# An eight-core block of convolution, attention and a product layer: work moved between the engines, and layer-norm sums made inside the tile loops

## The chip, the cores and the metric

The kernel runs on the 8 NeuronCores of one Trainium2 chip, each with its own part of the tokens and no traffic between cores. The metric is the device time of the slowest core, in microseconds (us). A core has TensorE (PE; its weight loads are PEld), VectorE (DVE), ScalarE (ACT), GpSimd (POOL) and SyncE (SP), each with its own queue that runs in program order; they wait for one another by semaphores only.

## What is computed

x has 4 x 2048 tokens of 4096 values. The reference, cut to what matters (all biases kept, names shortened):

```python
def attn(x):
    y = conv1d(x, conv_w, width=3, 'SAME') + conv_b        # 4096 -> 3*1024
    q, k, v = split(y, 3)                                  # in blocks of 128 tokens
    qh, kh, vh = q @ wq + bq, k @ wk + bk, v @ wv + bv     # 16 heads of 64
    p = softmax(where(causal, (qh/8) @ kh.T, -1e9))        # within a block
    return ((p @ vh) @ wo + bo) @ proj_w + proj_b          # -> 4096
def ffn(x):
    return x @ W.T + b + sum_e probs[e] * (x @ A[e].T) @ B[e].T   # 16 x rank 16
x = layernorm(x + attn(x))
x = layernorm(x + ffn(x))
```

## The kernel before

Each core takes 1024 tokens (T), held transposed: the 4096 channels are 32 chunks (DC) of 128 partitions, the tokens run along the free dimension in two halves of 512 (TH). All products are bf16, 128x128 weights against 128x512 data into one PSUM bank of eight; `tile_i % 8` picks the bank. Nothing orders the work but the program: `Sched.op` (line 65) appends an instruction to an engine's list with its semaphore waits, so the order in which the Python loops emit is the order of every queue. A DVE or ACT instruction also waits for its predecessor on its own engine. DMAs are issued from POOL (they cast float32 to bf16 on the way) or from SP.

The stages, in order:

- **Convolution** (lines 290 to 337), q/k/v products (349 to 416) and a pre-pass for the softmax maxima (427 to 472). The change leaves these alone.
- **Attention** (474 to 547), eight blocks of 128 tokens, PSUM halves psA and psB in turn. `attn_smm(b)` makes the scores. `attn_chain(b)`: ACT exp (497), DVE mask multiply (501), PE sums by a matmul with ones (507), DVE reciprocal over 128x2048 (513), PE p times v (521), and 16 small DVE multiplies that scale by the reciprocal and write otb (539). Emission is smm(0), smm(1), chain(0), smm(2), chain(1) and so on; smm(b+2) waits for the last otb write of block b, and lies ahead of the ones matmul of block b+1 in PE's queue.
- **P4**, `emit_p4(half)` (560 to 687): 8 tiles of otb times wo (592), then 32 tiles of a1b times proj_w (665), 8 matmuls each. Weights come tile by tile into two buffers, wsA and wsB, by POOL DMA (627); the load of tile n+2 waits for the matmuls of tile n. x comes as float32 into xjit0/1 by SP DMA (643). DVE adds bias and x while it reads PSUM and writes res1 in bf16 (676).
- **LN1**: `emit_ln1_stats` (689): 32 ACT squares (703), and two matmuls with ones for each chunk, the sum (709) and the sum of squares (716). `emit_ln_chain` (726): three ACT instructions, a DVE subtract and a reciprocal, an ACT square root. `emit_ln1_apply` (751): for each chunk a DVE add and a DVE multiply, 64 in all, with float32 negmean and rstd.
- **ht**, `emit_ht(half)` (762): 64 matmuls with A (772), and two DVE evacuations to hb (782).
- Emission around LN1 is p4(0), stats(0), apply(0), the POOL loads of A and B (806, 810), p4(1), ht(0), stats(1), apply(1), ht(1).
- **FFN** (867 to 906): 64 tiles of 34 matmuls (878, 887); DVE adds bias and x1 from PSUM (896); weights by POOL DMA (859).
- **LN2** (919 to 979), for each half in turn: squares (935), ones matmuls (941, 950), the chain, then 32 times a DVE add (967), a DVE multiply (970) and an SP DMA to the output (974), through four ob buffers.

In P4 the order within a tile is:

```python
        for dmc in range(DC):
            ...                       # waits: pw_ld[dmc], a1_done, bank_free[bank]
            for wc in range(WC): ...  # pmm, 8 matmuls on PE
            stream_free[par] = ("tC", S.n("tC"))
            ...
            S.op("vector", pevac, wait=ww)   # ww: the matmuls and xj_ld[dmc]
            if dmc + 2 < DC:
                emit_pw_load(dmc + 2)
                emit_xj_load(dmc + 2)
```

Of the kernel before, what the change touches and what calls it, by code (L numbers as in the profile page):

```python
# [14 lines left out]
D = 4096  # L15
# [35 lines left out]
OFF_SPARE = 206656  # L51


class Sched:
# [41 lines left out]
def build_nc(taps=(), stop_after='full'):  # L96
# [25 lines left out]
    idf_d = dt("idf", (128, 128), F32)  # L122

# [8 lines left out]
    def sb(name, off, shape, dtype):  # L132
# [25 lines left out]
    rstd = sb("rstd", OFF_STATS + 6144, (128, TH), F32)  # L158
    hb = sb("hb", OFF_HBOX, (128, 2048), BF16)
# [29 lines left out]
    xjit0 = sb("xjit0", REG2 + 40960, (128, TH), F32)  # L189
    xjit1 = sb("xjit1", REG2 + 43008, (128, TH), F32)  # L190
# [14 lines left out]
    SEMS = ("xS", "c0", "c1", "w2", "s0", "s1", "sD",  # L205
# [30 lines left out]
    v_prep = S.n("vC")  # L236

# [254 lines left out]
    def attn_chain(b):  # L492
# [8 lines left out]
        S.op("vector", lambda e, pb=pb: e.tensor_mul(  # L501
            pb[:, :], pb[:, :], maskt[:, :]),
            wait=[("cC", st["exp"])])
        st["mask"] = S.n("vC")
        for j in range(4):
            def lmm(e, j=j, ps=ps, pb=pb):
                return e.matmul(ps[:, j * 512:(j + 1) * 512], ones128[:, :],  # L507
                                pb[:, j * 512:(j + 1) * 512],
                                start=True, stop=True)
            S.op("tensor", lmm, wait=[("vC", st["mask"])],  # L510
                 inc="tC" if j == 3 else None)
# [3 lines left out]
        st["recip"] = S.n("vC")  # L515
        for h in range(H):
# [9 lines left out]
            S.op("tensor", omm, wait=[("vC", st["recip"])],  # L526
                 inc="tC" if h == H - 1 else None)
        st["omm"] = S.n("tC")
        for h in range(H):
            def oev(e, b=b, h=h, ps=ps, lv=lv):  # L530
                src = ps[(h % 2) * 64:(h % 2) * 64 + 64,
                         (h // 8) * 512 + ((h // 2) % 4) * 128:
                         (h // 8) * 512 + ((h // 2) % 4) * 128 + 128]
                dst = otb[(h % 2) * 64:(h % 2) * 64 + 64,
                          (h // 2) * 1024 + b * 128:
                          (h // 2) * 1024 + b * 128 + 128]
                lvs = lv[(h % 2) * 64:(h % 2) * 64 + 64,
                         scol(h):scol(h) + 128]
                return e.tensor_mul(dst, src, lvs)  # L539
            S.op("vector", oev, wait=[("tC", st["omm"])])  # L540
        blk_oevac[b] = [("vC", S.n("vC"))]
# [7 lines left out]
    p3_done = [("cC", S.n("cC")), ("vC", S.n("vC")), ("tC", p3_t_done)]  # L549
# [9 lines left out]

    def emit_p4(half):  # L560
        nonlocal tile_i
        hofs = half * TH
        wo_ld = {}
        def emit_wo_load(wc):
# [3 lines left out]
            waits = [("tC", p3_t_done)]  # L568
# [13 lines left out]
        for wc in range(WC):  # L582
            par = wc % 2
            buf = wsA if par == 0 else wsB
            bank = tile_i % 8
# [28 lines left out]
        xj_free = {0: None, 1: None}  # L614

# [15 lines left out]
        def emit_xj_load(dmc):  # L631
# [14 lines left out]
            S.op("sync", xdma, wait=xw, inc=sem, k=16)  # L646
# [6 lines left out]
        res1_writes = []  # L653
        for dmc in range(DC):
# [3 lines left out]
            bank = tile_i % 8  # L658
# [3 lines left out]
            for wc in range(WC):  # L662
                def pmm(e, dmc=dmc, wc=wc, bank=bank, buf=buf,
                        first=(wc == 0), last=(wc == WC - 1)):
# [3 lines left out]
                        start=first, stop=last)  # L668
                S.op("tensor", pmm, wait=waits,
                     inc="tC" if wc == WC - 1 else None)  # L670
                waits = []
            stream_free[par] = ("tC", S.n("tC"))
            t_grp = S.n("tC")
            ww = [("tC", t_grp), xj_ld[dmc]]
            def pevac(e, dmc=dmc, bank=bank, xbuf=xbuf):
                return e.scalar_tensor_tensor(
                    res1_ap(dmc), pbank(bank), projb[:, dmc:dmc + 1],
                    xbuf[:, :], ALU.add, ALU.add)
            S.op("vector", pevac, wait=ww)
            bank_free[bank] = ("vC", S.n("vC"))  # L680
            xj_free[par] = ("vC", S.n("vC"))
            res1_writes.append(S.n("vC"))
# [4 lines left out]
        ln_state[half] = dict(res1=res1_writes)  # L687

    def emit_ln1_stats(half):
        nonlocal tile_i  # L690
        st = ln_state[half]
        b1 = tile_i % 8
        b2 = (tile_i + 1) % 8
        tile_i += 2
        w1 = [bank_free[b1]] if b1 in bank_free else []
        w2w = [bank_free[b2]] if b2 in bank_free else []
        mm2_done = []
        for dc in range(DC):
            sqw = [("vC", st["res1"][dc])]
            if dc >= 2:  # L700
                sqw.append(("tC", mm2_done[dc - 2]))
            def sq(e, dc=dc):
                return e.activation(  # L703
                    sqtmp[:, (dc % 2) * 512:(dc % 2) * 512 + 512],
                    res1_ap(dc), AF.Square)
            S.op("scalar", sq, wait=sqw)
            c_sq = S.n("cC")
            def mm1(e, dc=dc, b1=b1):
                return e.matmul(pbank(b1), ones128[:, :], res1_ap(dc),
                                start=(dc == 0), stop=(dc == DC - 1),  # L710
                                skip_group_check=True)
# [12 lines left out]
        st["b1"], st["b2"], st["t_stats"] = b1, b2, t_stats

    def emit_ln_chain(st):
# [4 lines left out]
        S.op("scalar", lambda e: e.activation(  # L731
            negmean[:, :], pbank(b1), AF.Copy, bias=0.0, scale=-1.0 / D),
# [13 lines left out]
        S.op("scalar", lambda e: e.activation(rstd[:, :], tmp1[:, :],  # L746
                                              AF.Sqrt),
             wait=[("vC", v_r)])
        return S.n("cC")

    def emit_ln1_apply(half):
        st = ln_state[half]
        c_rstd = emit_ln_chain(st)
        for dc in range(DC):
            S.op("vector", lambda e, dc=dc: e.tensor_add(
                res1_ap(dc), res1_ap(dc), negmean[:, :]),
                wait=[("cC", c_rstd)])
            S.op("vector", lambda e, dc=dc, half=half: e.tensor_mul(  # L758
                x1b_ap(half, dc), res1_ap(dc), rstd[:, :]))
        st["applied"] = ("vC", S.n("vC"))  # L760

    def emit_ht(half):
        nonlocal tile_i
        for erc in range(ERC):
            bank = tile_i % 8
            waits = [g_at, ln_state[half]["applied"]]
# [292 lines left out]
```

How the kernel before makes its waits and increments, by code:

```python
        def run(e, sems, fn=fn, waits=waits, inc=inc, k=k):  # L85
            for s, v in waits:
                e.wait_ge(sems[s], v)
            inst = fn(e)
            if inc is not None:
                inst.then_inc(sems[inc], k)
```

## Time and profile before

| | us |
|---|---|
| runs of the kernel before, median of 3 | 2531.28 (2527.34 to 2542.32) |
| the profiled execution, whole | 2560.23 |
| its span on the slowest core (core 7) | 2558.7 |
| spans of the other cores | 2512.8 to 2541.9 |

| stage on core 7 | from, to (us) | length |
|---|---|---|
| convolution, q/k/v, pre-pass | 0 to 1247.5 | 1247.5 |
| attention | 1247.5 to 1443.7 | 196.2 |
| P4 of half 0 (wo; proj_w) | 1443.7 to 1619.8 | 30.9; 145.2 |
| statistics of half 0, wait for weights | 1619.8 to 1648.0 | 28.2 |
| P4 of half 1 (wo; proj_w) | 1648.0 to 1831.0 | 31.0; 152.0 |
| ht(0), LN1 of half 1, ht(1) | 1831.0 to 1945.0 | 114.0 |
| FFN | 1945.0 to 2415.7 | 470.7 |
| LN2 | 2415.7 to 2558.7 | 143.0 |

The page gives PE 76% of the span busy, DVE 19%, ACT 6%, POOL 13%. A row of the timeline is a start, a length, the engine, the line of the kernel, the operation with the names and shapes that it writes and reads, and how many instructions are merged; the bracket tells how long the engine had stood idle and what released it. A matmul's length includes its way through the array, so back-to-back matmuls overlap: 32 of them that last 0.38 us each take 6.9 us. The clock column is the granted TensorE clock as a share of full speed: 1.00 is 2.4 GHz, 0.50 is 1.2 GHz, a value between is a mixture over the stretch.

### The profile page before, as it was taken

To read this page: it belongs to the slowest core of one execution; us is meant where nothing else is said; L and a number is where in the kernel's file an instruction comes from. 1 tells how busy PE (TensorE), PEld (TensorE's weight loads), DVE (VectorE), ACT (ScalarE), POOL (GpSimd) and SP (SyncE) were. 2 spreads that over 40 slices of the span, in tenths; PEclk is the share of its full clock that TensorE was granted. 3 is DMA by queue.
4 is the path that set the end of the run, shared out by engine and by line. 5 is a ranking of instruction groups with operands and counts; after the bars stand their busy time and mean duration, and the time that the engine had idled before them with its cause. 6 is when DMAs were issued, how large, how long until landed. Compare 5 with 4: busy or idle time off the path is not lost.

```text
span 2558.7 us, 20840 instructions; the slowest of 8 cores (2512.8 to 2558.7 us)
## 1 busy us (share of the span) xinstructions
PE 1951.9 (76%) x8634; PEld 831.3 (32%) x8634; DVE 485.8 (19%) x586; ACT 163.6 (6%) x234; POOL 324.1 (13%) x316
## 2 busy tenths in 40 slices
PE   0499999999999999999311355665618999999940
PEld 0244444444444444444200111121203444444300
DVE  0000000000000000001687411261161011011077
ACT  0000000000000000012000000300120000000140
POOL 1112112121121212100000111111100111111000
PEclk9988899999999999999655678877868999999975
DMA  9956888898979797910000378978702878778433
GB/s 144 97 54 57 76 82 78 83 84 77 90 75 96 66 89 66 83 33 1 1 0 0 41 107 115 118 96 121 93 0 24 75 66 74 74 67 76 40 119 144
DMA packets 544385, 184.51 MB, mean 72 GB/s; under 512 B 516131, under 2 KB 520355, under 8 KB 544036
## 3 DMA queue, kind: packets, MB, share of 16 engines
q0 software_dynamic: 524416, 148.93, 60.9%
q1 hardware_dynamic: 19876, 34.25, 4.4%
q8 instruction: 69, 1.13, 0.2%
q14 instruction: 24, 0.20, 0.0%
HBM read 315.29 MB, written 16.78 MB: 130 GB/s over the span
## 4 chain that ended last, share of the span: by engine, by line
PE 71%; DVE 13%; DMA 10%; issue 5%; ACT 1%; POOL 0%; DVEq 0%; POOLq 0%; ACTq 0%
PE psA L304 20%; PE psB L304 20%; PE psA L878 9%; PE psB L878 9%; DVE linv L513 4%; DMA wsB<-projw 3%; DMA wsA<-projw 3%; DMA wsA<-wo 2%; PE psB L665 2%; PE psA L665 2%; DVE ob L967 2%; DVE ob L970 2%; DVE otb L539 1%; PE psA L361 1%; PE psB L361 1%
## 5 line engine op out<-in xcount | busy, mean ns | idle before, releaser
L304 PE MATMUL psA<-xb,cwb 128*128 128x512 bf16 x2304 | 521.8, 391 | 96.3 <-DMA cwb<-cw 96.3
L304 PE MATMUL psB<-xb,cwb 128*128 128x512 bf16 x2304 | 517.0, 388 | 0.0
L304 PEld LDWEIGHTS psA<-xb,cwb 128*128 128x128 bf16 x2304 | 228.7, 99 | 388.0 <-issue 168.5
L304 PEld LDWEIGHTS psB<-xb,cwb 128*128 128x128 bf16 x2304 | 227.6, 99 | 288.4 <-issue 59.2
L267 POOL DMA_DIRECT2D cwb<-cw x144 | 164.8, 1175 | 879.1 <-PE psA L304 436.1
L326 DVE TENSOR_SCALAR qkvb<-psA,convb_s 128x512 bf16<-128x512 f32 x8 | 6.0, 750 | 588.0 <-PE psA L304 588.0
L326 DVE TENSOR_SCALAR qkvb<-psB,convb_s 128x512 bf16<-128x512 f32 x8 | 6.0, 751 | 505.5 <-PE psB L304 505.5
L859 POOL DMA_DIRECT2D wsA<-Wt x32 | 36.5, 1146 | 304.8 <-PE psA L887 213.2
L665 PE MATMUL psB<-a1b,wsA 128*128 128x512 bf16 x128 | 45.3, 518 | 36.8 <-DMA wsA<-projw 35.2
L665 PE MATMUL psA<-a1b,wsB 128*128 128x512 bf16 x128 | 46.1, 525 | 30.3 <-DMA wsB<-projw 30.3
L665 PE MATMUL psA<-a1b,wsA 128*128 128x512 bf16 x128 | 41.1, 479 | 34.8 <-DMA wsA<-projw 33.4
L665 PE MATMUL psB<-a1b,wsB 128*128 128x512 bf16 x128 | 38.8, 457 | 28.8 <-DMA wsB<-projw 28.7
L703 ACT ACTIVATE sqtmp<-res 128x512 bf16<-128x512 bf16 x64 | 40.3, 629 | 317.9 <-PE psA L716 138.5
L859 POOL DMA_DIRECT2D wsB<-Wt x32 | 36.5, 1144 | 190.2 <-PE psA L887 100.7
L878 PE MATMUL psA<-x1bA,wsB 128*128 128x512 bf16 x256 | 56.6, 379 | 1.1 <-DVE res_lo L896 1.1
L878 PE MATMUL psA<-x1bA,wsA 128*128 128x512 bf16 x256 | 56.6, 379 | 1.1 <-DVE hb L782 1.1
L878 PE MATMUL psB<-x1bA,wsB 128*128 128x512 bf16 x256 | 56.6, 379 | 0.0
L878 PE MATMUL psB<-x1bA,wsA 128*128 128x512 bf16 x256 | 56.6, 379 | 0.0
L935 ACT ACTIVATE sqtmp<-res_lo 128x512 bf16<-128x512 bf16 x32 | 20.1, 629 | 543.0 <-PE psA L950 449.1
L772 PE MATMUL psB<-x1bB_lo,atb 128*128 128x512 bf16 x32 | 9.5, 461 | 58.7 <-DVE x1bB_hi L758 58.7
L513 DVE RECIPROCAL linv<-psA 128x2048 f32<-128x2048 f32 x4 | 51.8, 12957 | 8.7 <-PE psA L507 8.7
L513 DVE RECIPROCAL linv<-psB 128x2048 f32<-128x2048 f32 x4 | 51.8, 12957 | 8.7 <-PE psB L507 8.7
(169 smaller groups left out, 1505.8 us busy)
## 6 DMA issues: line engine op xcount, KB each, us to landing
cwb<-cw POOLq DMA_DIRECT2D x144, 512.0 KB, 21.6
xjit<-xT SPq DMA_DIRECT2D x64, 256.0 KB, 3.9
wsA<-Wt POOLq DMA_DIRECT2D x32, 512.0 KB, 10.4
wsB<-Wt POOLq DMA_DIRECT2D x32, 512.0 KB, 10.4
outT<-ob SPq DMA_DIRECT2D x64, 256.0 KB, 2.0
xb<-xT POOLq DMA_DIRECT2D x4, 2052.0 KB, 46.3
wsA<-projw POOLq DMA_DIRECT2D x32, 256.0 KB, 5.7
wsB<-projw POOLq DMA_DIRECT2D x32, 256.0 KB, 5.7
```

The lines of the kernel that those rows point to most:

```text
L267: return e.dma_start(out=dst, in_=src)
L304: return e.matmul(pbank(bank), buf[:, (w * 32 + dc) * 128:(w * 32 + dc + 1) * 128], xb[:, dc * (T + 2) + tokc * 512 + w: dc * (T + 2) + to ...
L361: return e.matmul(pbank(bank), wcs[dc][:, hc * 128:hc * 128 + 128], qkvb[:, (qoff + dc) * 1024 + tokc * 512: (qoff + dc) * 1024 + tokc * 5 ...
L513: S.op("vector", lambda e, ps=ps, lv=lv: e.reciprocal(lv[:, :], ps[:, :]), wait=[("tC", st["lmm"])])
L539: return e.tensor_mul(dst, src, lvs)
L665: return e.matmul(pbank(bank), buf[:, wc * 128:wc * 128 + 128], a1b[:, wc * TH:(wc + 1) * TH], start=first, stop=last)
L703: return e.activation(sqtmp[:, (dc % 2) * 512:(dc % 2) * 512 + 512], res1_ap(dc), AF.Square)
L859: return e.dma_start(out=dst, in_=src)
L878: return e.matmul(pbank(bank), buf[:, dc * 128:dc * 128 + 128], x1b_ap(half, dc), start=first, stop=False)
L935: return e.activation(sqtmp[:, (dc % 2) * 512:(dc % 2) * 512 + 512], res2_ap(dc)[:, hofs:hofs + TH], AF.Square)
L967: S.op("vector", lambda e, dc=dc, slot=slot, hofs=hofs: e.tensor_add(ob[slot][:, :], res2_ap(dc)[:, hofs:hofs + TH], negmean[:, :]), wait=ww)
L970: S.op("vector", lambda e, slot=slot: e.tensor_mul(ob[slot][:, :], ob[slot][:, :], rstd[:, :]))
```

## The change

- Attention: the mask multiply goes from DVE to POOL. After the reciprocal a new POOL multiply scales the 128x2048 probabilities, and p times v waits for it; the 16 DVE writes of otb become 4 ACT copies of 64x512 each.
- P4: x is loaded as bf16 by POOL DMA and added by a ninth matmul with an identity (idb, a new constant). ACT instead of DVE evacuates PSUM. The square and the two ones matmuls of a chunk are emitted right behind its evacuation, so in PE's queue they stand ahead of the next tile's matmuls. `emit_ln1_stats` is gone. Tiles rotate over banks 0 to 3; banks 4 and 5 hold the sums. The first weight and x loads wait for earlier blocks of the attention than before.
- LN1 apply: negmean and rstd are cast to bf16, and 16 DVE instructions on 128x2048 (the row repeated 4 times by `bc3`) take the place of 64 on 128x512.
- FFN: an identity matmul adds x1; ACT evacuates and squares; both ones matmuls stand in PE's queue behind each tile (banks 4 to 7). The first two weight loads are emitted ahead of ht(1).
- LN2: both chains first; then chunk by chunk half 0 on DVE and half 1 on POOL, two ob buffers each; the output DMAs stand in SP's queue in turn.
- POOL instructions wait for their predecessor by a semaphore of their own (gC). The `stop_after` exits are removed.

```diff
+def bc3(ap2d, reps):
+    return dataclasses.replace(ap2d, ap=[ap2d.ap[0], [0, reps], ap2d.ap[1]])
@@ attn_chain
-        S.op("vector", lambda e, pb=pb: e.tensor_mul(
+        S.op("gpsimd", lambda e, pb=pb: e.tensor_mul(
             pb[:, :], pb[:, :], maskt[:, :]),
+            wait=[("cC", st["exp"])], inc="gC")
@@ after the reciprocal
+        S.op("gpsimd", lambda e, pb=pb, lv=lv: e.tensor_mul(
+            pb[:, :], pb[:, :], lv[:, :]),
+            wait=[("vC", st["recip"])], inc="gC")
+        st["pnorm"] = ("gC", S.n("gC"))
-            S.op("tensor", omm, wait=[("vC", st["recip"])],
+            S.op("tensor", omm, wait=[st["pnorm"]],
-        for h in range(H):
-            def oev(...): ... return e.tensor_mul(dst, src, lvs)
-            S.op("vector", oev, wait=[("tC", st["omm"])])
-        blk_oevac[b] = [("vC", S.n("vC"))]
+        for g in range(2):
+            for bot in range(2):
+                def oev(...): ... return e.activation(dst, src, AF.Copy)
+                S.op("scalar", oev, wait=[("tC", st["omm"])])
+        blk_oevac[b] = [("cC", S.n("cC")), ("vC", st["recip"])]
@@ emit_p4
-            S.op("sync", xdma, wait=xw, inc=sem, k=16)
+            S.op("gpsimd", xdma, wait=xw, inc=sem, k=16)
+            def pxadd(e, dmc=dmc, bank=bank, xbuf=xbuf):
+                return e.matmul(pbank(bank), idb[:, :], xbuf[:, :],
+                                start=False, stop=True)
+            S.op("tensor", pxadd, wait=[xj_ld[dmc], sd_idb], inc="tC")
             stream_free[par] = ("tC", S.n("tC"))
-            S.op("vector", pevac, wait=ww)
+            S.op("scalar", pevac, wait=pw_)
             if dmc + 2 < DC:
                 emit_pw_load(dmc + 2)
                 emit_xj_load(dmc + 2)
+            S.op("scalar", sq, wait=sqw)
+            S.op("tensor", mm1, wait=stat_w1 + [("cC", c_evac)], ...)
+            S.op("tensor", mm2, wait=stat_w2 + [("cC", c_sq)], inc="tC")
@@ emit_ln1_apply
-        for dc in range(DC):
-            S.op("vector", ... tensor_add(res1_ap(dc), res1_ap(dc), negmean))
-            S.op("vector", ... tensor_mul(x1b_ap(half, dc), res1_ap(dc), rstd))
+        gate = emit_ln_chain(st, negmean, rstd, make_bf=True)
+        for g in range(8):
+            S.op("vector", lambda e, r=r: e.tensor_add(
+                r, r, bc3(nmb[:, :], 4)), wait=[gate])
+            S.op("vector", lambda e, r=r, xo=xo: e.tensor_mul(
+                xo, r, bc3(rstdb[:, :], 4)))
@@ FFN tile
+            S.op("tensor", fxadd, wait=[sd_idb], inc="tC")
-            S.op("vector", fevac, wait=[("tC", t_grp)])
+            S.op("scalar", fevac, wait=[("tC", t_grp)])
+            S.op("scalar", sq2, wait=sqw)
+            S.op("tensor", mm1, wait=hs["w"][hs["b1"]] + [("cC", c_evac)], ...)
+            S.op("tensor", mm2, wait=hs["w"][hs["b2"]] + [("cC", c_sq)],
+                 inc="tC")
@@ LN2
+    for half in range(2):
+        gate = emit_ln_chain(st, nm_t, rs_t, make_bf=False)
+        apply_specs.append((half, nm_t, rs_t, gate))
+    for dc in range(DC):
+        for half, nm_t, rs_t, gate in apply_specs:
+            slot = (dc % 2) * 2 + half
+            eng = "vector" if half == 0 else "gpsimd"
+            ...                       # app1: add negmean, app2: times rstd
             S.op("sync", sdma, wait=[v_ap], inc=osem, k=16)
```

## Rows read from the trace of the kernel before

**Rows 1.** Busy by stage: stretch, length, PE, PEld, DVE, ACT, POOL, clock, DMA, GB/s

```profile
1247.50:1443.70 196.20, 31.55 (x288) 16.76 (x288) 150.39 (x145) 15.74 (x8) 1.75 (x2) 0.50 0.04 6
1474.60:1619.80 145.20, 82.08 (x256) 27.95 (x257) 23.27 (x31) 1.26 (x2) 29.88 (x34) 0.81 0.80 112
1679.00:1831.00 152.00, 87.08 (x257) 28.63 (x258) 43.59 (x61) 1.56 (x3) 29.38 (x33) 0.77 0.84 114
1945.00:2415.70 470.70, 469.60 (x2176) 212.73 (x2177) 47.29 (x63) 1.26 (x2) 68.44 (x60) 1.00 0.73 67
2415.70:2447.00 31.30, 19.28 (x67) 4.51 (x65) 5.42 (x4) 21.93 (x35) 0.00 (x0) 0.90 0.00 1
```

**Rows 2.** Timeline, one attention block: start, length, engine, line, operation

```profile
1267.55 1.06 PE L521 MATMUL psA<-pb,vtb 128*64 128x128 bf16 x16 [13.28 <-DVE linv L513]
1268.79 6.17 DVE L539 TENSOR_TENSOR otb<-psA,linv 64x128 bf16<-64x128 f32 x16 [1.38 <-PE psA L521]
1275.06 1.23 DVE L501 TENSOR_TENSOR pb<-pb,maskt 128x2048 bf16<-128x2048 bf16 x1
1276.30 1.97 ACT L497 ACTIVATE pb<-psA,gneg 128x2048 bf16<-128x2048 f32 x1 [23.38 <-PE psA L484]
1276.43 1.87 PE L507 MATMUL psB<-pb,ones_s 128*128 128x512 bf16 x4 [0.29 <-DVE pb L501]
1278.48 12.96 DVE L513 RECIPROCAL linv<-psB 128x2048 f32<-128x2048 f32 x1 [2.19 <-PE psB L507]
```

**Rows 3.** Groups by line and shape: busy us, mean ns, idle before

```profile
L602 ACT ACTIVATE a1b<-psA,bos 128x512 bf16<-128x512 f32 x8 | 5.5, 687 | 65.5 <-PE psA L592 65.5
L442 DVE TENSOR_REDUCE m1all<-psA 128x1 f32<-128x2048 f32 x4 | 9.2, 2292 | 1.3 <-PE psA L434 0.9
```

**Rows 4.** DMA issues of the page: KB each, median us to landing

```profile
xjit<-xT SPq DMA_DIRECT2D x64, 256.0 KB, 3.9
wsA<-projw POOLq DMA_DIRECT2D x32, 256.0 KB, 5.7
```

**Rows 5.** Timeline, two projection tiles and what follows the second

```profile
1478.60 1.89 PE L665 MATMUL psA<-a1b,wsB 128*128 128x512 bf16 x8 [0.60 <-DMA wsB<-projw]
1481.03 0.87 POOL L627 DMA_DIRECT2D wsB<-projw  x1 [1.61 <-PE psA L665]
...
1614.80 3.56 PE L665 MATMUL psB<-a1b,wsA 128*128 128x512 bf16 x8 [4.80 <-DMA wsA<-projw]
1614.99 1.67 POOL L806 DMA_DIRECT2D atb<-At  x1 [3.58 <-issue]
...
1648.00 2.29 PE L592 MATMUL psA<-otb,wsA 128*128 128x512 bf16 x5 [5.18 <-DMA wsA<-wo]
```

**Rows 6.** Timeline, statistics of half 0: squares, and a matmul that waits

```profile
1620.76 21.54 ACT L703 ACTIVATE sqtmp<-res 128x512 bf16<-128x512 bf16 x30 [138.50 <-PE psA L716]
1621.53 0.38 PE L716 MATMUL psA<-sqtmp,ones_s 128*128 128x512 bf16 x1 [0.28 <-ACT sqtmp L703]
```

**Rows 7.** Timeline, from projection of half 1 to the last product

```profile
1830.90 15.15 PE L772 MATMUL psA<-x1bA,atb 128*128 128x512 bf16 x64
1846.22 0.75 DVE L782 TENSOR_SCALAR hb<-psA,probs_s 128x512 bf16<-128x512 f32 x1 [6.16 <-PE psA L772]
...
1871.28 0.69 DVE L741 TENSOR_TENSOR tmp<-tmp,tmp 128x512 f32<-128x512 f32 x1 [24.31 <-ACT tmp L736]
1876.38 0.69 DVE L755 TENSOR_TENSOR res<-res,negmean 128x512 bf16<-128x512 bf16 x1 [0.95 <-ACT rstd L746]
...
1927.71 5.84 PE L772 MATMUL psB<-x1bB_lo,atb 128*128 128x512 bf16 x16 [58.73 <-DVE x1bB_hi L758]
1944.98 7.07 PE L878 MATMUL psA<-x1bA,wsA 128*128 128x512 bf16 x32 [1.08 <-DVE hb L782]
```

**Rows 8.** Timeline, last normalization of half 1: first step, first apply

```profile
2497.71 0.60 ACT L731 ACTIVATE negmean<-psA 128x512 f32<-128x512 f32 x1 [27.54 <-DVE ob L970]
2505.02 0.69 DVE L967 TENSOR_TENSOR ob<-res_lo,negmean 128x512 f32<-128x512 bf16 x1 [1.02 <-ACT rstd L746]
```

More of the change, by code:

```diff
@@ L69, in op @@
                 inc = "vC"
+        elif eng == "gpsimd":
+            wait = list(wait) + [("gC", self.n("gC"))]
+            if inc is None and k == 1:
+                inc = "gC"
         elif eng == "scalar":
@@ L236, in build_nc @@
     v_prep = S.n("vC")
+    S.op("sync", lambda e: e.dma_start(out=idb[:, :], in_=idb_d),
+         wait=[("vC", v_prep)], inc="sD", k=16)
+    sd_idb = ("sD", S.n("sD"))
     for i in range(4):
@@ L509, in lmm @@
                                 start=True, stop=True)
-            S.op("tensor", lmm, wait=[("vC", st["mask"])],
+            S.op("tensor", lmm, wait=[st["mask"]],
                  inc="tC" if j == 3 else None)
@@ L663, in pmm @@
                 def pmm(e, dmc=dmc, wc=wc, bank=bank, buf=buf,
-                        first=(wc == 0), last=(wc == WC - 1)):
+                        first=(wc == 0)):
                     return e.matmul(
@@ L764, in emit_ht @@
         for erc in range(ERC):
-            bank = tile_i % 8
-            waits = [g_at, ln_state[half]["applied"]]
+            bank = p45_bank(tile_i)
+            waits = [g_at] + ln_state[half]["applied"]
             if bank in bank_free:
@@ L884, in build_nc, with bmm @@
             for erc in range(ERC):
[L885 to L886 removed]
+                def bmm(e, oc=oc, erc=erc, bank=bank, half=half):
                     return e.matmul(
@@ L891, in bmm, with fxadd @@
                            erc * 1024 + half * TH + TH],
-                        start=False, stop=last)
-                S.op("tensor", bmm, inc="tC" if erc == ERC - 1 else None)
+                        start=False, stop=False)
+                S.op("tensor", bmm)
+            def fxadd(e, oc=oc, bank=bank, half=half):
+                return e.matmul(pbank(bank), idb[:, :], x1b_ap(half, oc),
+                                start=False, stop=True)
+            S.op("tensor", fxadd, wait=[sd_idb], inc="tC")
@@ new lines, in build_nc, with mm1 @@
+            sqw = []
+            if oc >= 1:
+                sqw.append(("tC", hs["mm2_done"][oc - 1]))
+            S.op("scalar", sq2, wait=sqw)
+            c_sq = S.n("cC")
+            def mm1(e, oc=oc, half=half, b1=hs["b1"]):
+                return e.matmul(pbank(b1), ones128[:, :],
+                                res2_ap(oc)[:, half * TH:half * TH + TH],
+                                start=(oc == 0), stop=(oc == DC - 1),
+                                skip_group_check=True)
+            S.op("tensor", mm1, wait=hs["w"][hs["b1"]] + [("cC", c_evac)],
+                 inc="tC" if oc == DC - 1 else None)
@@ new lines, in build_nc, with mm2 @@
+            hs["w"][hs["b1"]] = []
+            def mm2(e, oc=oc, half=half, b2=hs["b2"]):
+                return e.matmul(pbank(b2), ones128[:, :],
+                                sqtmp[:, half * 512:half * 512 + 512],
+                                start=(oc == 0), stop=(oc == DC - 1),
+                                skip_group_check=True)
+            S.op("tensor", mm2, wait=hs["w"][hs["b2"]] + [("cC", c_sq)],
+                 inc="tC")
+            hs["w"][hs["b2"]] = []
+            hs["mm2_done"].append(S.n("tC"))
```

317 lines of the change are left out of this document (132 added, 185 removed).

## The prediction

> **What bounds the kernel now.** I read the page first, then the busy time by stage, then the timeline of each stage that the change touches. The stages follow one another almost without overlap, so what the change does is a sum over stages. In the product stages PE is the limit: in FFN 2176 matmuls take 470.7 us, 0.216 us each, at a clock of 1.00 [rows 1]. In the attention no engine is: PE is busy 31.55 of 196.2 us and DVE 150.39; blocks run one after another on a chain through all of them [rows 1, 2]. In P4's projection PE is busy 82.08 of 145.2 us and waits for proj_w [rows 1, 5]. The three LN stretches hang on ACT and DVE. The reader should look for where the new queues put ACT or POOL between two pieces of PE's work.
>
> **Attention, +53.** Before, a block takes 24.03 us (first evacuation at 1268.79, next reciprocal at 1278.48, and so on round): p times v to evacuation 1.24, 16 evacuations 6.27, mask to the ones matmul 1.37, that to the reciprocal 2.05, reciprocal to p times v 13.1 [rows 2]. After, smm(b+2) still waits for the evacuation of block b. The exp of block b+1 now stands behind that evacuation in ACT's queue, and the mask behind the exp, so both join the chain. Round it goes: 1.24; four ACT copies, each 0.69 from the 128x512 evacuation plus 0.05 between, 3.0 [rows 3]; exp 1.97 plus 0.2; mask m; 0.14 and 2.05; reciprocal 12.96 and 0.15; scaling n; 0.12. That is 21.8 + m + n. No row shows POOL computing. The floor is the mask on DVE, 1.23 [rows 2]; the ceiling, the slowest pass over 128x2048, 12.96. I take 4.6 for either, twice a plain DVE pass over that shape, 2.29 [rows 3]: it is nearer to an elementwise pass than to the reciprocal, and I choose twice. One round is 31.0 against 24.03. Eight of them are 248, and they hold the exp and the mask of the first block, which 196.2 has beside its eight rounds (196.2 - 192.2 = 4.0); with 1 for the first scores (16 small matmuls, as the 1.06 [rows 2]) 249 - 196 = +53. The Trainium skill (GPSIMD Engine Reference, "Elementwise — side-by-side cycle accounting") gives 4,497 ns for a POOL tensor_tensor over 2048 float32, where DVE's takes 2,293. By that m + n is 9.0 and the term +52; no run here shows it yet.
>
> **P4, +22.** In PE's queue a tile is 8 matmuls, identity, ones matmul that waits for the evacuation, ones matmul that waits for the square, and only then the next tile. That PE does wait for an ACT square shows in the statistics now, 0.28 us idle before the one shown, ACT at 0.72 a square over 30 [rows 6]. From the identity's start: 0.38 for it, 0.17 to ACT, evacuation 0.69 [rows 3], 0.06, square 0.63, 0.14, last ones matmul 0.22: 2.29 us. The eight matmuls are 1.73 at full clock, 3.41 at half (their rows, 1.89 and 3.56, include the last one's way out) [rows 5], so the chain is 4.0 or 6.1 a tile (0.4 more on the slow matmuls). The weight buffers set another limit: 0.54 from the matmuls' end to the POOL issue, 5.7 to land [rows 4, 5], 0.1, and the nine matmuls 2.1 or 4.0, for two tiles: 4.2 or 5.2 a tile. So 4.2 at full clock (buffers) and 6.1 at half (chain). Now 32 tiles take 145.2 and 152.0, 4.54 and 4.75, at clocks of 0.81 and 0.77 [rows 1], that is at full clock 0.62 and 0.54 of the time. With those shares: 4.9 and 5.1, I take 5.0. Two halves: 320 - 297.2 = +23. The x loads now stand behind the second weight load in POOL's queue; the first lands 3.9 us after its issue [rows 4], some 2 us late for the first identity of each half: +4. Removing stats(0) gains nothing: between the halves PE waits for wo, queued behind A and B, issued at 1614.99 and usable at 1648.00 [rows 5]; that load starts a tile earlier, -3. In the attention's last block the evacuation is shorter than the wo load that it hid: -2. The x loads by POOL cost 64 issues of under 0.87 within tiles of 5 us, beside 0.87 for the weights: hidden; were PE faster, they would add at most 1.7 of 4.2.
>
> **LN1 of half 1, -51.** Now from the end of P4 (1831.0) to FFN (1944.98) 114 [rows 7]. After: tail of the last tile 1.5; ht(0) 15.1; its last DVE evacuation, which still stands ahead of the chain in DVE's queue, 0.9; subtract to first apply 5.1 [rows 7]; two casts, at 0.69 and a gap, 1.5; 16 applies at 1.23 [rows 2] plus 0.1, 21.3; ht(1) and its evacuation, 1927.71 to 1944.98, 17.3. Sum 62.7. The 1.23 is that of the mask, where all three operands are bf16, as here. If the repeated row costs that speed, the apply is at 2.29 [rows 3] and 17 dearer.
>
> **FFN, +147.** A tile is now 34 x 0.216 = 7.36. After it the identity starts, and 2.29 later, by the steps above, the next tile: 2.29 x 64 = +147. PE is still busy in four fifths of a tile, and in the statistics, where it is idle more than that, the clock stays at 0.90 [rows 1], so I leave it at full. DVE loses 64 evacuations, which were hidden and give nothing. Earlier weight loads: PE does not wait for them in FFN now (469.6 busy of 470.7) [rows 1], so nothing.
>
> **LN2, +14.** Now 143.0. After: no statistics. Chain 0 is 7.3 us from first ACT step to first apply [rows 8], chain 1 stands behind it on ACT and DVE, 0.4 before: 15.0. Then 32 chunks. DVE has two instructions, 1.59 together; POOL has two over 128x512 float32, each 1.38, twice DVE's 0.69 [rows 8], bounds 0.69 and, at a quarter of 12.96, 3.2. SP's queue takes the halves in turn and each half has two buffers, so the slower engine sets the pace: 2.76 a chunk if the engines work side by side, 4.35 if one waits while the other works. No row shows them both at it. I take the sum, 139.2, and keep the other for the range. With the last DMA, 2.5: 156.7. The Trainium skill (SBUF — State Buffer, "SBUF: two separate sides") says that a DVE instruction with two SBUF inputs and a POOL one that reads SBUF exclude each other for their whole length. That speaks against this part of the change and for the sum; the trace is silent.
>
> **Sum.** +53 +22 -51 +147 +14 = +185 us. The profiled execution took 2560.2 (span 2558.7), 29 above the median of the runs, and its working would end at 2745; on the median, 2531 + 185 = 2716 us. The convolution is the same in both.
>
> **The rivals.**
> - DVE and POOL do not hinder each other in LN2: 32 x (4.35 - 2.76) = 51 less, 2665. For it: the two engines have separate queues, and no row shows them waiting. Against it: the rule above.
> - POOL is as quick as DVE: mask 1.2 and scaling 2.3 save 5.7 x 8 = 46, LN2 at 3.2 a chunk saves 37: 2633. Only DVE's rows speak for it.
> - POOL is twice as slow as I take it: 9.2 x 8 = 74 and 2.76 x 32 = 88 more, 2878. Nothing speaks for it but the 12.96.
> - P4 runs at half clock throughout: 1.1 x 64 = 70 more, 2786. For it: PE stands idle twice in each tile; against it: it has 11 matmuls where it had 8.
> - Not slower: PE runs the next tile's matmuls while ACT evacuates and squares. Then an FFN tile costs three matmuls, 0.65, instead of 2.29, -106; P4 keeps full clock at 4.2, -51, and its tail goes, -4: 2555, within 1%. It decides once the stall is under some 0.4 us of the 1.64 a tile. Against it: PE waits for the square even now, with 30 more chunks emitted behind [rows 6].
>
> **How the numbers follow.** The forecast 0.58; no hindrance in LN2 0.12; P4 at half clock 0.10; quick POOL 0.08; slow POOL 0.06; no stall 0.03; the rest 0.03. The range 2650 to 2800 takes in the first three. One per cent is about what a measurement of this kernel can tell from no change. Of the rivals only the last ends within it, and faster needs it and a quick POOL together: faster 0.02, same 0.03, slower 0.95.
>
> **What would show it.** Tile starts in FFN 9.6 us apart with PE waiting for ACT twice in each; a block of the attention every 31 us with POOL 4.6 twice; tiles of P4 at 5.0; from P4 to FFN 63; the LN2 chunk at 4.35, with DVE waiting for POOL or longer. Wrong would be: FFN tiles at 8.0, POOL at 1.2 or 9, an apply at 2.3, or a clock below 0.9 in FFN.

## The result, and the profile after

| | before | after |
|---|---|---|
| median of 10 runs each, us | 2535.4 | 2645.2 |
| ratio | | 1.0435 (95% interval 1.0413 to 1.0457) |
| span of the profiled core, us | 2558.7 (core 7) | 2646.7 (core 4) |

The change makes the kernel 4.35% slower, 110 us. The forecast was 2716, 185 us more than before, with a range from 2650 to 2800: the direction was right, the size was not, and the measured time lies 5 us below the range. Three of the twenty executions took 8% longer at a lower granted clock; this ratio and those below leave such executions out.

The two profiled cores are not alike before the attention: core 7 of before reaches it at 1247.5 us, most other cores near 1209. The stages are therefore compared over all eight cores. Each is taken from the first matmul of a stage to the first of the next, on each core's own trace (LN2 of the changed kernel, which has no matmul, from the end of the last one), and the table has the median of the eight.

| stage | before | after | difference | forecast |
|---|---|---|---|---|
| convolution, q/k/v, pre-pass | 1209.2 | 1212.4 | +3 | 0 |
| attention | 196.1 | 240.5 | +44 | +53 |
| P4 of half 0, with what follows it | 206.3 | 199.9 | -6 | |
| P4 of half 1 | 180.4 | 176.5 | -4 | +22 for both |
| ht(0), LN1 of half 1, ht(1) | 112.5 | 59.9 | -53 | -51 |
| FFN | 469.7 | 617.2 | +147 | +147 |
| LN2 | 142.8 | 120.5 | -22 | +14 |

The differences add up to 109. The same stages on core 4, busy time by stage; the columns are those of [rows 1], in this order: the attention, the projections of half 0 and of half 1, LN1, FFN, and LN2's chains and its apply:

```profile
1213.60:1454.00 240.40, 30.00 (x284) 16.69 (x288) 103.66 (x8) 34.67 (x40) 66.79 (x18) 0.50 0.02 2
1487.30:1633.00 145.70, 93.78 (x335) 34.07 (x341) 0.00 (x0) 40.82 (x62) 46.66 (x64) 0.92 0.84 87
1697.00:1848.80 151.80, 96.28 (x337) 34.84 (x345) 0.00 (x0) 42.13 (x64) 46.69 (x64) 0.90 0.82 84
1848.80:1909.20 60.40, 30.51 (x127) 13.06 (x130) 27.50 (x24) 2.42 (x4) 0.91 (x1) 0.75 0.28 28
1909.20:2526.30 617.10, 528.31 (x2320) 228.73 (x2366) 0.00 (x0) 84.27 (x128) 68.44 (x60) 1.00 0.57 52
2526.30:2540.10 13.80, 0.10 (x1) 0.00 (x0) 8.09 (x4) 4.21 (x7) 0.00 (x0) 0.57 0.00 0
2540.10:2646.70 106.60, 0.00 (x0) 0.00 (x0) 95.19 (x64) 0.63 (x1) 94.02 (x64) 0.50 0.41 158
```

In FFN (617.10 us) PE is busy 528.31, where it was busy 469.60 of 470.70: standing still has grown by 88 us, and the busy time by 59, for more matmuls and for matmuls that start alone and so overlap with no other. The projection's clock is 0.92 and 0.90, against 0.81 and 0.77. A block of the attention in the timeline, to be held against [rows 2]:

```profile
1252.83 12.96 DVE L534 RECIPROCAL linv<-psB 128x2048 f32<-128x2048 f32 x1 [16.78 <-PE psB L528]
1270.22 1.06 PE L546 MATMUL psB<-pb,vtb 128*64 128x128 bf16 x16 [17.56 <-POOL pb L537]
1271.43 2.64 ACT L562 ACTIVATE otb<-psB 64x512 bf16<-64x512 f32 x4 [25.04 <-PE psB L546]
1274.17 1.97 ACT L518 ACTIVATE pb<-psA,gneg 128x2048 bf16<-128x2048 f32 x1
1276.34 4.05 POOL L522 TENSOR_TENSOR pb<-pb,maskt 128x2048 bf16<-128x2048 bf16 x1 [6.27 <-ACT pb L518]
1282.57 12.96 DVE L534 RECIPROCAL linv<-psA 128x2048 f32<-128x2048 f32 x1 [16.79 <-PE psA L528]
1295.73 4.08 POOL L537 TENSOR_TENSOR pb<-pb,linv 128x2048 bf16<-128x2048 bf16 x1 [15.35 <-DVE linv L534]
```

From one reciprocal to the next (1252.83 to 1282.57) are 29.74 us, against 24.03. The four ACT copies take 2.64, the exp follows behind them, the mask behind the exp, and the two POOL multiplies take 4.05 and 4.08.

### The profile page after: what moved, and what is told of

It is laid out like the page before. It is cut to its first block, busy times and chain, and to the rows that moved or that the text cites. A ratio compares the mean times of both kernels' runs of the same rounds, so it can differ in the third digit from the quotient of the medians.

```text
span 2646.7 us, 20307 instructions; the slowest of 8 cores (2612.3 to 2646.7 us)
## 1 busy us (share of the span) xinstructions
PE 1913.4 (72%) x8591; PEld 833.6 (31%) x8762; DVE 301.9 (11%) x166; ACT 270.4 (10%) x394; POOL 519.0 (20%) x460
## 3 DMA queue, kind: packets, MB, share of 16 engines
q8 instruction: 71, 1.16, 0.2%
## 4 chain that ended last, share of the span: by engine, by line
PE 67%; DMA 7%; POOL 7%; ACT 6%; DVE 6%; issue 6%; another core or an unknown queue 0%; ACTq 0%; POOLq 0%; DVEq 0%
PE psA L325 19%; PE psB L325 19%; PE psA L890 16%; DVE linv L534 4%; PE psA L698 3%; DMA wsB<-projw 2%; DMA wsA<-wo 2%; POOL ob L973 2%; POOL ob L969 2%; ACT sqtmp L921 2%; DMA wsA<-projw 1%; POOL pb L537 1%; POOL pb L522 1%; PE psA L815 1%; PE psA L382 1%
## 5 line engine op out<-in xcount | busy, mean ns | idle before, releaser
L325 PE MATMUL psA<-xb,cwb 128*128 128x512 bf16 x2258 | 498.4, 379 | 103.4 <-DMA cwb<-cw 100.9
L890 PE MATMUL psA<-x1bA,wsA 128*128 128x512 bf16 x496 | 112.1, 379 | 2.1 <-DVE hb L825 1.3
L890 PE MATMUL psA<-x1bA,wsB 128*128 128x512 bf16 x505 | 112.5, 379 | 0.4
L698 PE MATMUL psA<-a1b,wsB 128*128 128x512 bf16 x252 | 68.2, 416 | 14.6 <-DMA wsB<-projw 13.1
L698 PE MATMUL psA<-a1b,wsA 128*128 128x512 bf16 x252 | 70.8, 429 | 9.9 <-DMA wsA<-projw 8.3
L736 PE MATMUL psB<-res,ones_s 128*128 128x512 bf16 x62 | 23.9, 386 | 62.1 <-ACT res L714 62.1
L890 PEld LDWEIGHTS psA<-x1bA,wsA 128*128 128x128 bf16 x512 | 49.9, 98 | 59.1 <-issue 1.5
L890 PEld LDWEIGHTS psA<-x1bA,wsB 128*128 128x128 bf16 x512 | 49.9, 98 | 57.6
L714 ACT ACTIVATE res<-psA,projb_s 128x512 bf16<-128x512 f32 x64 | 44.0, 687 | 219.8 <-PE psA L705 214.6
L522 POOL TENSOR_TENSOR pb<-pb,maskt 128x2048 bf16<-128x2048 bf16 x8 | 32.4, 4044 | 160.2 <-ACT pb L518 160.2
```

The source lines that it names most:

```text
L325: return e.matmul(pbank(bank), buf[:, (w * 32 + dc) * 128:(w * 32 + dc + 1) * 128], xb[:, dc * (T + 2) + tokc * 512 + w: dc * (T + 2) + to ...
L522: S.op("gpsimd", lambda e, pb=pb: e.tensor_mul(pb[:, :], pb[:, :], maskt[:, :]), wait=[("cC", st["exp"])], inc="gC")
L698: return e.matmul(pbank(bank), buf[:, wc * 128:wc * 128 + 128], a1b[:, wc * TH:(wc + 1) * TH], start=first, stop=False)
L714: return e.activation(res1_ap(dmc), pbank(bank), AF.Identity, bias=projb[:, dmc:dmc + 1], scale=1.0)
L890: return e.matmul(pbank(bank), buf[:, dc * 128:dc * 128 + 128], x1b_ap(half, dc), start=first, stop=False)
```

## The experiments

Each starts from the changed kernel, 2645.2 us, and differs in the edit shown, if nothing else is said. Stage times are medians over eight cores, as above, from one profiled execution of each kernel.

### FFN: the sums one tile later

```diff
             S.op("tensor", fxadd, wait=[sd_idb], inc="tC")
             t_grp = S.n("tC")
+            while pend:              # ones matmuls of the tile before
+                pend.pop(0)()
...
-            S.op("tensor", mm1, ...); S.op("tensor", mm2, ...)
+            pend.append(sums)        # mm1 and mm2 of this tile
```

> The changed kernel with one edit: in FFN the two matmuls with ones of a tile are emitted behind the next tile's matmuls. Theory A, PE stands still while ScalarE evacuates and squares: a tile goes from 9.64 us to 37 x 0.216 = 8.0, FFN from 617 to 512, the whole from 2645 to about 2540, level with the kernel before. Theory B, the 147 us come from something that the order does not touch (the clock, the weight loads): FFN stays above 600.

Measured: 2545.9 us, 99 less and 1.0057 times the kernel before (1.0034 to 1.0080); FFN 512.3. First a tile of the changed kernel, then the same place here (timeline: start, length, engine, line):

```profile
1964.79 0.38 PE L906 MATMUL psA<-x1bB_lo,idb 128*128 128x512 bf16 x1
1965.32 0.69 ACT L911 ACTIVATE res_lo<-psA,ffnb_s 128x512 bf16<-128x512 f32 x1 [8.23 <-PE psA L906]
1966.10 0.63 ACT L921 ACTIVATE sqtmp<-res_lo 128x512 bf16<-128x512 bf16 x1
1966.15 0.38 PE L930 MATMUL psB<-res_lo,ones_s 128*128 128x512 bf16 x1 [0.98 <-ACT res_lo L911]
1966.87 0.38 PE L938 MATMUL psB<-sqtmp,ones_s 128*128 128x512 bf16 x1 [0.34 <-ACT sqtmp L921]
```

```profile
1964.24 0.38 PE L907 MATMUL psA<-x1bA,idb 128*128 128x512 bf16 x1
1964.45 0.38 PE L933 MATMUL psB<-res_lo,ones_s 128*128 128x512 bf16 x1
1964.67 0.38 PE L938 MATMUL psB<-sqtmp,ones_s 128*128 128x512 bf16 x1
1964.77 0.69 ACT L914 ACTIVATE res_lo<-psA,ffnb_s 128x512 bf16<-128x512 f32 x1 [6.58 <-PE psA L907]
```

In the first, PE stands 0.98 us until ACT has evacuated and 0.34 until it has squared; the bracket names ACT both times. In the second the identity and the two sums start 0.21 to 0.22 apart, with no bracket, and ACT evacuates and squares beside the next tile's matmuls. 105 of the 147 us are gone with the order of two matmuls. What is left, 42.6, is three more matmuls in each of 64 tiles: 64 x 3 x 0.216 = 41.5. Theory A, in its numbers.

### The attention: exp and mask of the next block first

```diff
+    attn_head(0)                     # head: exp and mask
     for b in range(1, NB):
         attn_smm(b)
-        attn_chain(b - 1)
+        attn_mid(b - 1)              # ones matmul, reciprocal
+        attn_head(b)
+        attn_tail(b - 1)             # scaling, p times v, evacuation
```

> The changed kernel with one edit: in the attention the exp and the mask multiply of block b+1 are emitted ahead of the scaling of block b, so ScalarE and GpSimd do them during block b's reciprocal. Theory A, exp (2.0 us) and mask (4.05 us) are on the chain of a block only because of ScalarE's queue order: a block goes from 29.74 us to about 24.3 (evacuation, scores, ones matmul, reciprocal, scaling, p times v), the attention from 240 to about 202, the whole to about 2605. Theory B, a block is bound by VectorE and GpSimd getting in each other's way: it stays above 28 us, or the reciprocal grows beyond 12.96 where it lies beside the mask.

Measured: 2610.9 us, 34 less; attention 200.2, which is 40 less. P4 of half 0, whose code is the same, took 210.6 where it took 199.9; why is not known. Timeline:

```profile
1263.88 1.97 ACT L518 ACTIVATE pb<-psB,gneg 128x2048 bf16<-128x2048 f32 x1 [1.44 <-PE psB L505]
1265.72 12.96 DVE L540 RECIPROCAL linv<-psA 128x2048 f32<-128x2048 f32 x1 [11.57 <-PE psA L534]
1266.05 4.04 POOL L522 TENSOR_TENSOR pb<-pb,maskt 128x2048 bf16<-128x2048 bf16 x1 [7.62 <-ACT pb L518]
1278.88 4.08 POOL L549 TENSOR_TENSOR pb<-pb,linv 128x2048 bf16<-128x2048 bf16 x1 [8.79 <-DVE linv L540]
1290.25 12.96 DVE L540 RECIPROCAL linv<-psB 128x2048 f32<-128x2048 f32 x1 [11.57 <-PE psB L534]
```

Reciprocals start 24.53 us apart. Exp and mask now lie beside the reciprocal, which keeps its 12.96, so POOL reading SBUF did not slow a DVE instruction that reads PSUM. 40 of the 44 us were the queue order of ACT. With exp and mask out of the chain a block is within 0.5 us of the 24.03 before: the scaling by POOL costs about what the shorter evacuation saves.

### The attention of the kernel before

```diff
-        S.op("gpsimd", ... tensor_mul(pb, pb, maskt)), S.op("gpsimd", ... tensor_mul(pb, pb, lv))
+        S.op("vector", ... tensor_mul(pb, pb, maskt))
-        4 x S.op("scalar", oev)
+        16 x S.op("vector", oev)
```

> The changed kernel with the attention of the kernel before (mask and evacuation on VectorE, no scaling by GpSimd). If the stages add up, the attention is back at 196 from 240 and the whole at 2601, 44 less; P4 of half 0 starts from the old hand-over, which may move it by 5.

Measured: 2597.8 us, 47 less; attention 196.1, which is 44 less, P4 of half 0 201.9 against 199.9. The stages add up to within 5 us.

### LN2: VectorE alone, GpSimd alone

```diff
-            eng = "vector" if half == 0 else "gpsimd"
+            eng = "vector"
```

> The changed kernel with one edit: in LN2 VectorE does both halves, GpSimd none. Theory A, VectorE and GpSimd take turns there, so that the second engine brings nothing: 64 pairs at 1.59 us are 102 against 103 now, the whole within 3 us of 2645. Theory B, they do work side by side: LN2 grows from 120 to more than 150.

Measured: 2647.6 us; LN2 119.1 against 120.5. With GpSimd alone (half 0 is copied by ScalarE and not normalized):

```diff
             if eng == "vector":
-                S.op("vector", app1, wait=ww)
-                S.op("vector", app2)
+                S.op("scalar", ... e.activation(ob[slot], res2_ap(dc), AF.Copy), wait=ww)
```

> The changed kernel; in LN2 half 0 is not normalized, ScalarE copies it (that part of the computation is left out), so GpSimd works with VectorE idle. Theory A, the 1.42 and 1.53 us of a GpSimd instruction contain waiting for VectorE: alone it takes about 1.26, as the very last one does, a chunk 2.8 and LN2 106. Theory B, no waiting: 1.45 and a chunk 3.2 as now.

Measured (one time, without an interval): 2628.8 us; LN2 104.3. Timelines of LN2, first the changed kernel, then VectorE alone, then GpSimd alone:

```profile
2549.22 1.53 POOL L973 TENSOR_TENSOR ob<-ob,rstd 128x512 f32<-128x512 f32 x1
2549.73 1.57 DVE L973 TENSOR_TENSOR ob<-ob,rstd 128x512 f32<-128x512 f32 x1
2550.89 1.42 POOL L969 TENSOR_TENSOR ob<-res_lo,nm 128x512 f32<-128x512 bf16 x1
2551.40 1.46 DVE L969 TENSOR_TENSOR ob<-res_lo,negmean 128x512 f32<-128x512 bf16 x1
```

```profile
2601.91 0.69 DVE L969 TENSOR_TENSOR ob<-res_m,negmean 128x512 f32<-128x512 bf16 x1
2602.71 0.69 DVE L973 TENSOR_TENSOR ob<-ob,rstd 128x512 f32<-128x512 f32 x1
2603.50 0.69 DVE L969 TENSOR_TENSOR ob<-res_m,nm 128x512 f32<-128x512 bf16 x1
```

```profile
2562.08 1.16 POOL L969 TENSOR_TENSOR ob<-res_lo,nm 128x512 f32<-128x512 bf16 x1
2563.38 1.26 POOL L973 TENSOR_TENSOR ob<-ob,rstd 128x512 f32<-128x512 f32 x1
2564.79 1.16 POOL L969 TENSOR_TENSOR ob<-res_lo,nm 128x512 f32<-128x512 bf16 x1
```

A DVE instruction takes 0.69 us alone and 1.46 or 1.57 beside POOL; one of POOL takes 1.16 or 1.26 alone and 1.42 or 1.53 beside DVE. So each holds the other up, and the second engine brings nothing: a chunk (both halves) takes 3.23 us shared and 3.18 on DVE alone. But they do not exclude each other for their whole length. The four instructions of a chunk, by their lengths alone, are 0.69 + 0.69 + 1.16 + 1.26 = 3.80, and the chunk is 3.23: at least 0.57 of it is done side by side. (With its pauses DVE's pair is 1.59 and POOL's 2.70, together 4.29; but one engine's pause can be filled by the other even if instructions exclude each other.) The rule of the Trainium skill (SBUF — State Buffer, "SBUF: two separate sides"), an exclusive hold for the whole instruction, has the direction right and is too strong here. The trace of the changed kernel also shows who waits: at the start of LN2, on all eight cores, a DVE multiply that began 0.03 us ahead of POOL's first add kept its 0.69, and that add took 1.68 instead of 1.16. Which part of an instruction holds the other up was not tried.

### P4: the sums one tile later, and behind the loop

```diff
             S.op("tensor", pxadd, wait=[xj_ld[dmc], sd_idb], inc="tC")
+            while pend4:             # ones matmuls of the tile before
+                pend4.pop(0)()
```

> The changed kernel with one edit: in P4 the two matmuls with ones are emitted behind the next tile's matmuls. Theory A, a P4 tile was bound by PE's wait for ScalarE (4.02 us at full clock): without it the weight buffers bind at 4.1 to 4.2, so P4 stays as it is within 10 us and the whole within 10 us of 2645. Theory B, what made P4 quicker than forecast is the clock (0.90 to 0.92 against 0.77 to 0.81 before) and nothing else: the clock should stay at 0.9 here too, since the matmuls are the same.

```diff
-            (sq, mm1, mm2 within the loop over dmc)
+        for dmc in range(DC):        # after it
+            (sq, mm1, mm2)
```

> The changed kernel with squares and sums of P4 behind its loop, as before; ScalarE's evacuation and the identity matmul stay. Theory A, the two ones matmuls a tile are what holds the granted clock at 0.90: the clock of the projection falls to about 0.8 and a tile goes from 4.3 us to 4.5 or more, 25 us for the two halves of statistics come on top in half 1. Theory B, it is the x load and the evacuation that made the tiles quicker: the clock falls, the tile stays below 4.3.

Measured: 2663.4 us and 2686.4 us. From the first to the last projection matmul of a half, and its granted clock:

| | half 0, clock | half 1, clock |
|---|---|---|
| kernel before | 146.7, 0.81 | 148.1, 0.76 |
| changed kernel | 140.9, 0.95 | 142.1, 0.93 |
| sums one tile later | 150.8, 0.87 | 145.2, 0.89 |
| sums behind the loop | 159.4, 0.80 | 153.7, 0.80 |

The same matmuls, without the waits for ACT, are slower: 18 us in all. The length of one half is a weak witness, since the nine kernels of this document with the P4 of the changed kernel have 137.5 to 150.3 in half 0; but both halves of P4 with what follows them are 392.0 against 376.5, and none of the nine has more than 384.2 or a clock under 0.92. Theory A of the first expectation missed its 10 us, theory B its clock. Of the second expectation, theory A held: the clock fell to 0.80, and P4 of half 1 took 209.0, 32 more than in the changed kernel. But the clock fell with the sums still in the loop, too, when they only stood elsewhere. The POOL issues of the weights, changed kernel first, with the two sums of a tile, and the sums one tile later second, with one matmul of the latter:

```profile
1546.49 0.89 POOL L660 DMA_DIRECT2D wsA<-projw  x1 [2.60 <-PE psA L705]
1550.51 0.89 POOL L660 DMA_DIRECT2D wsB<-projw  x1 [2.60 <-PE psA L705]
1550.94 0.38 PE L736 MATMUL psB<-res,ones_s 128*128 128x512 bf16 x1 [0.98 <-ACT res L714]
1551.66 0.38 PE L743 MATMUL psB<-sqtmp,ones_s 128*128 128x512 bf16 x1 [0.35 <-ACT sqtmp L727]
1554.54 0.89 POOL L660 DMA_DIRECT2D wsA<-projw  x1 [2.60 <-PE psA L705]
```

```profile
1541.63 0.90 POOL L660 DMA_DIRECT2D wsB<-projw  x1 [1.81 <-PE psB L743]
1547.07 0.90 POOL L660 DMA_DIRECT2D wsA<-projw  x1 [4.00 <-PE psB L743]
1552.76 0.90 POOL L660 DMA_DIRECT2D wsB<-projw  x1 [4.25 <-PE psA L706]
1555.66 0.90 POOL L660 DMA_DIRECT2D wsA<-projw  x1 [1.46 <-PE psB L743]
1557.59 1.89 PE L699 MATMUL psA<-a1b,wsB 128*128 128x512 bf16 x8 [2.06 <-DMA wsB<-projw]
```

With the waits, tiles follow each other every 4.03 us here, and the load of each weight tile is issued 4.03 us behind the last and lands in time. Without them PE runs through a tile and then waits 2 to 3 us for weights, in three of the four tiles of this stretch; the issues come 5.4, 5.7 and 2.9 us apart, and the page's median from issue to landing rises from 5.3 and 5.5 to 5.8 and 6.3. In the projection of half 0 PE waits 42 us for ACT and 13 for weights in the changed kernel (core 4), and 0 and 55 here (core 1). The pause moved from ACT to the DMA, and the clock fell.

How much is the clock and how much the weights can be told in part from the 496 tile lengths of all eight cores. The changed kernel has 414 tiles wholly at full clock, 4.20 us on average (median 4.03), and 82 others, 6.07. With the sums one tile later there are 264 at full clock, 4.41, and 232 others, 5.12. The means are 4.51 and 4.74; with the changed kernel's share of full-clock tiles the second would be 4.53, an estimate from these numbers. So what the waits for ACT gave up came back as waits for weights, and the loss came with the clock. Without sums in the loop PE has still less to do, and clock and tile (5.0 and 4.8 us) are near the forecast's 4.9 and 5.1. What lowered the clock, the longer pauses or the unevenness, these runs do not tell.

### P4: four buffers

```diff
             buf = wsA if par == 0 else wsB
-            sem = "s0" if par == 0 else "s1"
+            sub = ((dmc // 2) % 2) * 1024           # two tiles in each buffer
+            sem = f"s{dmc % 4}"
...                                                  # the same for x: xjits[dmc % 4]
-            if dmc + 2 < DC: emit_pw_load(dmc + 2); emit_xj_load(dmc + 2)
+            if dmc + 4 < DC: emit_pw_load(dmc + 4); emit_xj_load(dmc + 4)
```

> The changed kernel with P4's sums deferred by one tile and with four weight and four x buffers in place of two. Theory A, a P4 tile is bound by the way of a weight tile through two buffers (issue, 5.3 to 6.3 us to land, matmuls): with four the loads run ahead and a tile falls from 4.4 us to below 4, the two projections from 286 us to about 240, the whole from 2645 to about 2600. Theory B, the DMA engines are full (their share is 0.82 to 0.84 there): a tile stays above 4.2.

This kernel also has the sums one tile later, so it is to be held against that one, 2663.4. Measured: 2592.6 us, 71 less than that and 53 less than the changed kernel; the projections 122.0 and 116.2, a tile 3.8 and 3.6. DMA issues, changed kernel first (KB each, median us to landing):

```profile
wsA<-projw POOLq DMA_DIRECT2D x32, 256.0 KB, 5.3
xjit<-xT POOLq DMA_DIRECT2D x64, 128.0 KB, 5.3
```

```profile
wsA<-projw POOLq DMA_DIRECT2D x32, 256.0 KB, 11.4
xjit<-xT POOLq DMA_DIRECT2D x64, 128.0 KB, 11.3
```

A load now takes twice as long to land, 11.4 us, with twice as many under way, and the tile is shorter all the same, at a clock of 0.89 in both halves. The two buffers were the limit, not the capacity of the DMA engines: on the slowest core their share (the time of all packets over the time of 16 engines) rose from 0.84 and 0.82 to 1.13 and 1.07. What four buffers bring with the sums left where they were was not tried.

### Towards a better kernel

> The changed kernel with FFN's sums deferred by one tile and the attention of the kernel before. If the stages add up: 2645 - 105 - 44 = 2496, 1.5% faster than the kernel before; what is left of the change is then P4, LN1 and LN2.

> As the one before, and FFN's evacuation is again on VectorE with x1 added there, so the identity matmul goes: 64 x 0.216 = 14 less, FFN 498 and the whole 2482, if the identity matmul costs its full 0.216 once PE no longer waits.

> As the one before, with another attention: exp and mask of the next block ahead (as in the exp experiment), the column sums made by weights of 64 columns so that they fill 128 partitions x 1024 instead of 128 x 2048, the reciprocal over those 1024 alone, one VectorE multiply of 128x1024 as evacuation, no scaling by GpSimd. The chain of a block: 1.24 + 1.3 + 0.1 + 0.95 + 2.04 + 6.6 + 0.1 = 12.4 us, the attention 107 against 196, the whole about 2393. If the sums or the evacuation cost more there, the block shows it.

> The version with the compact attention (2388 us) with P4's four weight and four x buffers and its deferred sums. If the two gains add up, 53 less: 2335, 8% faster than the kernel before. If the P4 gain of the single experiment came from something in the changed attention or FFN, it is smaller here.

The first has the sums of FFN one tile later and the attention of the kernel before; the second adds the `scalar_tensor_tensor` of the kernel before in FFN. The third has the emission order of the exp experiment, leaves the scaling by POOL out, and has these sums and this evacuation:

```diff
-                return e.matmul(ps[:, j * 512:(j + 1) * 512], ones128[:, :], ...)
+                p0 = (j // 2) * 64
+                return e.matmul(ps[p0:p0 + 64, (j % 2) * 512:(j % 2) * 512 + 512],
+                                ones128[:, 0:64], ...)
-            e.reciprocal(lv[:, :], ps[:, :])
+            e.reciprocal(lv[:, 0:1024], ps[:, 0:1024])
+            e.tensor_mul(otb[... 8 chunks of 128], ps[:, 0:1024], lv[:, 0:1024])
```

| | time, us | ratio to before | stage that moved |
|---|---|---|---|
| FFN's sums later, attention of before | 2490.6 (profiled execution) | | attention 196.1, FFN 512.3 |
| FFN evacuated by VectorE | 2478.4 (profiled execution) | 0.977 (0.974 to 0.980) | FFN 498.7 |
| compact attention | 2387.7 | 0.9409 (0.9381 to 0.9437) | attention 96.5 |
| and P4 with later sums and four buffers | 2334.5 | 0.9189 (0.9156 to 0.9222) | P4 182.4 and 151.1 |

For the first there is no ratio with an interval; its stages agree with the expectation. The last is 8.1% faster than the kernel before. P4's two edits together bring the same 53 us as in the changed kernel. The attention of the third was expected at 107 us and 12.4 a block; it took 96.5. Its edits were made together, and what each brings was not tried alone. A block of the compact attention:

```profile
1233.58 6.56 DVE L542 RECIPROCAL linv<-psB 128x1024 f32<-128x1024 f32 x1 [2.37 <-PE psB L535]
1241.52 1.22 DVE L569 TENSOR_TENSOR otb<-psB,linv 128x1024 bf16<-128x1024 f32 x1 [1.39 <-PE psB L556]
1243.86 1.07 PE L535 MATMUL psA<-pb,ones_s 128*64 128x512 bf16 x4
1245.11 6.56 DVE L542 RECIPROCAL linv<-psA 128x1024 f32<-128x1024 f32 x1 [2.36 <-PE psA L535]
1246.25 4.05 POOL L522 TENSOR_TENSOR pb<-pb,maskt 128x2048 bf16<-128x2048 bf16 x1 [7.49 <-ACT pb L518]
1251.81 1.06 PE L556 MATMUL psA<-pb,vtb 128*64 128x128 bf16 x16 [6.89 <-DVE linv L542]
1253.06 1.22 DVE L569 TENSOR_TENSOR otb<-psA,linv 128x1024 bf16<-128x1024 f32 x1 [1.39 <-PE psA L556]
```

Reciprocals start 11.5 us apart. The reciprocal over 1024 columns takes 6.56, half of 12.96, and one multiply of 1.22 does what 16 did in 6.17.

## Why the prediction was wrong, by its steps

- **FFN, +147: right**, to the microsecond and for the reason given. The clock stayed at 1.00. Moving the sums took away 105, which is the stall, 1.64 x 64.
- **LN1, -51: right.** Measured -53. The apply runs at 1.23 us with the repeated row, and ht(0)'s evacuation does stand ahead of the chain; the two casts took 0.43 each where 0.69 was taken.
- **Attention, +53: mechanism right, price too high.** "I take 4.6 for either" should have been 4.05 and 4.08, and the four copies took 2.64 where 3.0 was written. A round is 29.74, not 31.0; +44.
- **P4, +22: wrong.** The mechanism held: tiles wholly at full clock have a median of 4.03 us (the chain was to be 4.0) and a mean of 4.20 (the buffers were to set 4.2), and the eight tiles wholly at half clock a median of 6.13 (6.1). The step that failed is "with those shares: 4.9 and 5.1": it carried the share of time at full clock over from the kernel before, 0.62 and 0.54, though a tile has 11 matmuls where it had 8. The granted clock was 0.95 and 0.93, which is shares of 0.90 and 0.86, and the sum of the prediction with these gives 4.4 and 4.5 a tile; the tiles were 4.4. The text named the 11 matmuls, against the rival of half clock, and did not use them in the sum. It costs 32 us.
- **LN2, +14: wrong.** POOL's price was right (1.38 each taken; alone 1.16 and 1.26, and 0.14 between). The step that failed is "I take the sum, 139.2" with 4.35 a chunk. The chunk took 3.23, and LN2 is 22 shorter. Of the 1.12 between them some 0.5 are pauses between one engine's own instructions, which the other can fill even if the instructions exclude each other (4.29 with the pauses, 3.80 without), and 0.57 is work side by side. It costs 36 us, the largest part. The text had only the two ends, 2.76 and 4.35, and leaned on a rule where no row spoke. The middle of the two, 3.55, would have taken 26 us off the forecast, by luck, since nothing in the text spoke for it.
- Together these are 9 + 32 + 36 = 77 us; the forecast was 75 too high, and the rest is in the small stages (the convolution's +3, LN1's -2) and in rounding. All three misses have the same sign, and the range was made from single rivals, none of which had two of them at once.
- Of the rivals, none came about; LN2 without hindrance would have been 2.76 a chunk, and it lies between that and the sum. "PE runs the next tile's matmuls while ACT evacuates" was refuted by the changed kernel's own tiles, and made true on purpose by the first experiment.

## What to carry to other kernels

Where PE is the limit, emit a reduction that rides along in a loop one tile later than the data it reads: in FFN two small matmuls cost 1.64 us of waiting a tile on top of 0.43 of work. Look first at what PE will wait for next: in P4 the same move cost 18 us, since the weights came no sooner, and a gain came only together with four buffers. Before an instruction is given to an idle engine, look at what stands behind it in that engine's queue, and not at how busy the engine is; ACT was 6% busy in the kernel before, and its order alone cost 40 us in the attention. And where PE waits for loads while loads wait for PE's matmuls to free a buffer, try more buffers: here the landing time doubled, and the tile still went from 4.7 and 4.5 us to 3.8 and 3.6.

## What the runs showed of the hardware that was not expected

- VectorE and GpSimd on float32 tensor-tensor work in SBUF at once: 0.69 becomes 1.46 to 1.57 and 1.16 to 1.26 becomes 1.42 to 1.53; together no quicker than VectorE alone (3.23 and 3.18 us for the same work).
- GpSimd takes 4.05 us for a bf16 product of 128x2048 and 4.08 with one float32 input, where VectorE takes 1.23 for the first.
- Short, regular pauses of PE (0.98 and 0.34 us in a tile of 4.03) went with a granted clock of 0.93 to 0.95; pauses of 2 to 3 us with the same matmuls, with 0.87 to 0.89. The same matmuls with four buffers also had 0.89, at tiles of 3.8 and 3.6 us.
